# Moving the query, key and value loads of a routed-attention kernel from SyncE's queue to GpSimd's

## What is computed

```python
# layer 1: 3x3 convolution, 64 -> 64, activations quantized to 3 bits, weights to their sign
xq = round(min(1, |x|) * 7) / 7;  wq = sign(W) * mean(|W|);  x = conv(xq, wq) + b
# layer 2: attention over regions, then an MLP
q, k, v = split(layernorm(x) @ wqkv + bqkv)      # as 49 regions of 64 pixels
logits = mean(q over region) @ mean(k over region).T
idx = top_k(logits, 4)                           # 4 regions for each region
kg, vg = k[idx], v[idx]                          # 256 keys and values per region
out = softmax(qh @ kg.T / sqrt(8)) @ vg          # 8 heads of 8 channels
x = x + out @ wo + bo
x = x + gelu(layernorm(x) @ w1 + bm1) @ w2 + bm2
```

## Time and profile before

| | |
|---|---|
| median of 3 runs | 6373.1 us |
| the profiled execution | 6382.89 us |
| its span, first to last instruction | 6381.1 us |
| mean granted TensorE clock | 0.829 |
| busy: TensorE, VectorE, ScalarE, GpSimd | 80%, 57%, 51%, 43% |
| transfers: engines' mean busy share, rate | 31% (SyncE's queue), 81 GB/s |

### The profile page before, as it was taken

How to read it: one execution, slowest core, us unless ns; L and a number is a source line. 1 busy time by engine, 2 the same in 40 slices (tenths; PEclk the granted TensorE clock), 3 DMA queues, 4 the chain that set the end, 5 groups by cost and what they waited for, 6 DMA issues and landing times.

```text
span 6381.1 us, 185291 instructions
## 1 busy us (share of the span) xinstructions
PE 5098.8 (80%) x43666; PEld 3276.5 (51%) x43666; DVE 3650.2 (57%) x8855; ACT 3285.2 (51%) x6282; POOL 2765.1 (43%) x9656
## 2 busy tenths in 40 slices
PE   3488888887878888788788888888888888888888
PEld 1355555555555555555555555555555555555564
DVE  2356565565656565565555655656565555656555
ACT  1246455464555545455464554645455464554646
POOL 1345344353444435444353444535444353443543
PEclk9688788888888788888887888888788887888869
DMA  2433332333334233332333323323242333423311
GB/s 74 96 94 78 82 96 70 92 86 81 85 76 106 66 87 76 85 99 61 99 78 80 94 69 99 81 79 87 74 108 65 87 78 82 104 64 95 85 28 32
DMA packets 832787, 519.79 MB, mean 81 GB/s; under 512 B 592336, under 2 KB 830032, under 8 KB 831600
## 3 DMA queue, kind: packets, MB, share of 16 engines
q1 hardware_dynamic: 831600, 506.70, 31.1%
HBM read 268.80 MB, written 237.63 MB: 79 GB/s over the span
## 4 chain that ended last, share of the span: by engine, by line
PE 35%; SPq 18%; issue 14%; POOL 9%; POOLq 7%; DMA 6%; DVE 4%; DVEq 3%; ACT 2%; ACTq 0%
PE ps L970 9%; PE ps L1000 6%; PE ps L984 5%; SPq L262 5%; POOLq L223 4%; PE ps L863 4%; SPq L292 4%; POOL vg L480 4%; SPq L345 3%; DMA qm<-qk_d 3%; DVEq L223 3%; POOL kg L465 2%; PE ps L956 2%; DMA xin<-in_x 2%; POOL xin L492 2%
## 5 line engine op out<-in xcount | busy, mean ns | idle before, releaser
L705 DVE TENSOR_REDUCE mx<-ps 128x4 f32<-128x1024 f32 x1568 | 1921.7, 1226 | 2055.6 <-PE ps L970 1917.7
L816 ACT ACTIVATE pt<-ps 128x512 f32<-128x512 f32 x3136 | 1696.8, 593 | 1251.9 <-PE ps L984 1229.0
L480 POOL COPY vg<-vs 64x72 f32 x6272 | 1545.6, 246 | 1373.8 <-POOL kg L465 1104.7
L970 PE MATMUL ps<-kg,qm 96*128 96x256 f32 x6272 | 1430.3, 357 | 717.0 <-DMA qm<-qk_d 373.1
L970 PEld LDWEIGHTS ps<-kg,qm 96*128 96x128 f32 x6272 | 1027.4, 220 | 1520.4 <-issue 1361.0
L465 POOL CAST kg<-ks 96x128 fp32r x3136 | 852.1, 296 | 1880.2 <-POOL vg L480 779.6
L984 PE MATMUL ps<-qm,kg 97*128 97x256 f32 x6272 | 1192.9, 318 | 198.6 <-DMA qm<-max_d 143.4
L1000 PE MATMUL ps<-pt,vg 128*32 128x128 f32 x25088 | 1180.4, 312 | 39.4 <-DVE um L695 24.6
L984 PEld LDWEIGHTS ps<-qm,kg 97*128 97x128 f32 x6272 | 1013.4, 222 | 255.5 <-issue 152.0
L1000 PEld LDWEIGHTS ps<-pt,vg 128*32 128x32 f32 x25088 | 673.8, 120 | 306.0 <-issue 91.6
L616 DVE CAST kg<-ks 96x128 fp32r x3136 | 614.1, 237 | 127.0 <-issue 120.5
(11 more groups left out here) (113 smaller groups left out, 4147.5 us busy)
## 6 DMA issues: line engine op xcount, KB each, us to landing
qk_d<-stg SPq DMA_DIRECT2D x448, 224.0 KB, 3.1
qm<-qk_d SPq DMA_DIRECT2D x1792, 42.0 KB
ks<-qk_d SPq DMA_DIRECT2D x224, 336.0 KB, 3.6
vs<-v_d SPq DMA_DIRECT2D x448, 126.0 KB, 3.5
qk_d<-stg SPq DMA_DIRECT2D x112, 448.0 KB, 2.9
xin<-in_x SPq DMA_DIRECT2D x119, 224.0 KB, 2.6
xi_d<-xi SPq DMA_DIRECT2D x112, 224.0 KB, 2.3
max_d<-tr SPq DMA_DIRECT2D x1568, 2.0 KB
```

The lines of the kernel that those rows point to most:

```text
L480: j = pool.tensor_copy(vg[slot][rows, (k // 2) * VW:(k // 2 + 1) * VW], vs[place(m)[0]][rows, bass.ds(region, 1), :].rearrange("p o n -> p ...
L705: v.tensor_reduce(mx[h % 2][:].rearrange("p (g j e) -> p g j e", g=2, j=2)[:, :, :, 0], ps[:, 0:2, :].rearrange("p g (j k) -> p g j k", j= ...
L816: act.activation(pt[m % 2][:, c], ps[:, 2 + c, :], ACT.Exp, scale=float(HD) ** -0.5).then_inc(S["pt_ready"], 1)
L970: i = pe.matmul(ps[:, g, 256 * j:256 * j + 256], qm[c % 2][0:NP3, t, g, 2 * j:2 * j + 2, :].rearrange("p h t -> p (h t)"), kg[slot][0:NP3, ...
```

## The change

- All query, key and value loads move from SyncE's program to GpSimd's: a function `loads`, called at the end of GpSimd's step behind its keys, values and quantization. The queries keep their places (t = 3, 4, 5; 3, 3 and 2 transfers) and their wait.
- Keys and values of an image are 3 + 2 long transfers in place of 7 + 14: the keys one for each of the three terms, the values one for each half of the partitions. One goes out every second step, image 0's from h = 70, image 1's from h = 104. The waits in front of them (all staged, all gathered) move to GpSimd too; SyncE keeps the one before the routing indices, a step earlier.
- `v_d` is laid out by image. Staging is 3 transfers for queries and keys (the slots are taken by high, low and high part) and 4 for values (image by half), over four steps: 2, 2, 2, 1 (offsets 7 to 10).
- The semaphore `staged` becomes `qk_staged`, for which ScalarE waits as before, and `v_staged`, for which VectorE now waits at offset 6 before it overwrites `vstg`.
- In the prologue GpSimd issues the first 8 query loads and the first 5 key and value loads.

```diff
-A_LOAD, B_LOAD = 68, 2
-STAGE_DMAS = 7
-KV_DMAS = 3 * NW
+A_LOAD, B_LOAD = 70, 6
+QK_DMAS, V_DMAS = 3, 4
+KV_DMAS = 5
...
-        v_d = dram("v_d", (PAIRS, RT, R, 2, VW))
+        v_d = dram("v_d", (PAIRS, 2, RT, R, VW))
...
+        def gathered(eng, p, m):
+            for name in ("kd_ready", "kp_ready", "vg_ready"):
+                eng.wait_ge(S[name], p * STEPS + m)
+                settled(eng)
+        def queries(eng, q, c, heads):
+            i, s = c // NW, c % NW
+            src = qk_d[bass.ds(q, 1), i, 0:C, :, ST * s:ST * s + ST].rearrange("o (g h d) q (s t) -> g h (o d q) s t", g=NG, h=HG, s=NW)
+            for g, h in heads:
+                eng.dma_start(qm[c % 2][24 * h:24 * h + 24, :, g, h, :].bitcast(F32), src[g, h]).then_inc(q_loaded[c % 2], 16)
+        def keys_values(eng, q, i, n):
+            if n < 3:
+                src = qk_d[bass.ds(q, 1), i, C:2 * C, n // 2, :].rearrange("o (g c) n -> (o c) g n", g=NG)
+                dst = ks[i][n:NP3:3].rearrange("p g r t -> p g (r t)").bitcast(F32)
+            else:
+                src = v_d[bass.ds(q, 1), i].rearrange("o t r n -> (o t) (r n)")
+                dst = vs[i][64 * (n - 3):64 * (n - 3) + 64].rearrange("p r n -> p (r n)")
+            eng.dma_start(dst, src).then_inc(kv_loaded[i], 16)
+        def loads(eng, p, h, kind):
+            t, c = h % NW, h // NW
+            if t in (3, 4, 5) and live((c + 1) * NW, kind):
+                if t == 3 and not (kind == "lead" and c < 1):
+                    eng.wait_ge(S["st_full"], (p * STEPS + c * NW) * 2)
+                    settled(eng)
+                queries(eng, p + (c + 1) // 14, (c + 1) % 14, [(g, h) for g in range(NG) for h in range(HG)][(t - 3) * 3:(t - 2) * 3])
+            if kind == "loop":
+                if h == A_LOAD:
+                    staged_all(eng, p + 1)
+                    gathered(eng, p, R)
+                if 0 <= h - A_LOAD < 2 * KV_DMAS and (h - A_LOAD) % 2 == 0:
+                    keys_values(eng, p + 1, 0, (h - A_LOAD) // 2)
+            local = h if kind == "lead" else h - STEPS
+            if local >= 0 and kind != "last":
+                if local == B_LOAD and kind != "lead":
+                    gathered(eng, p, STEPS)
+                if 0 <= local - B_LOAD < 2 * KV_DMAS and (local - B_LOAD) % 2 == 0:
+                    keys_values(eng, p if kind == "lead" else p + 1, 1, (local - B_LOAD) // 2)
+        def first_loads(eng):
+            staged_all(eng, 0)
+            queries(eng, 0, 0, [(g, h) for g in range(NG) for h in range(HG)])
+            for n in range(KV_DMAS):
+                keys_values(eng, 0, 0, n)
+        def staged_all(eng, q):
+            eng.wait_ge(S["qk_staged"], (q + 1) * (16 * QK_DMAS * NW))
+            settled(eng)
+            eng.wait_ge(S["v_staged"], (q + 1) * (16 * V_DMAS * NW))
+            settled(eng)
...
-                    def part(term, rows, low):
-                        dst = qk_d[bass.ds(q, 1), :, rows, term, cut].rearrange("o i c n -> (o c) i n")
-                        sp.dma_start(dst, stg[rows, low].bitcast(F32)).then_inc(S["staged"], 16)
...
+                    def part(slot, rows, low):
+                        dst = qk_d[bass.ds(q, 1), :, 0:rows, slot, cut].rearrange("o i c n -> (o c) i n")
+                        sp.dma_start(dst, stg[0:rows, low].bitcast(F32)).then_inc(S["qk_staged"], 16)
+
+                    def value(i, half):
+                        dst = v_d[bass.ds(q, 1), i, :, NW * k + half:NW * k + NW:2].rearrange("o t r n -> (o t) r n")
+                        sp.dma_start(dst, vstg[64 * half:64 * half + 64, 0:4 - half, i, :]).then_inc(S["v_staged"], 16)
...
                     if off == 7:
                         sp.wait_ge(S["l_ready"], q * (2 * NW) + 2 * k + 2)
                         settled(sp)
-                        part(0, slice(0, 2 * C), 0)
-                        part(1, slice(0, C), 0)
-                        part(1, slice(C, 2 * C), 1)
+                        part(0, 2 * C, 0)
+                        part(1, 2 * C, 1)
                     if off == 8:
-                        part(2, slice(0, C), 1)
-                        part(2, slice(C, 2 * C), 0)
+                        part(2, C, 0)
                         sp.wait_ge(S["v_ready"], q * NW + k + 1)
                         settled(sp)
-                        value(0)
+                        value(0, 0)
                     if off == 9:
-                        value(1)
-
-            def staged_all(q):
-
-                sp.wait_ge(S["staged"], (q + 1) * (16 * STAGE_DMAS * NW))
-                settled(sp)
+                        value(0, 1)
+                        value(1, 0)
+                    if off == 10:
+                        value(1, 1)
...
+                loads(pool, p, h, kind)
...
+                first_loads(pool)
...
+                        if not (isinstance(n, int) and n == 0):
+                            v.wait_ge(S["v_staged"], n * (16 * V_DMAS))
                         v.wait_ge(S["v_full"], n + 1)
...
-                            act.wait_ge(S["staged"], n * (16 * STAGE_DMAS))
+                            act.wait_ge(S["qk_staged"], n * (16 * QK_DMAS))
```

More of the change, by code:

```diff
@@ L49 @@
 ROUTE_AT = 62
-A_LOAD, B_LOAD = 68, 2
-STAGE_DMAS = 7
-KV_DMAS = 3 * NW
+A_LOAD, B_LOAD = 70, 6
+QK_DMAS, V_DMAS = 3, 4
+KV_DMAS = 5
 def p_item(h):
-    return [(k, h - P_AT - P_EVERY * k) for k in range(NW) if 0 <= h - P_AT - P_EVERY * k <= 9]
+    return [(k, h - P_AT - P_EVERY * k) for k in range(NW) if 0 <= h - P_AT - P_EVERY * k <= 10]
 def f_item(h):
@@ L168, in build @@
             xq_done xq_ready conv_full xi_ready center_full sq_ready var_full lnv_ready rs_ready xh_ready rx_ready
-            qk_full h_ready l_ready v_full v_ready xi_stored staged
+            qk_full h_ready l_ready v_full v_ready xi_stored qk_staged v_staged
             reg_full reg_ready logit_full lg_ready top_ready topi_ready
@@ L255, in load_x @@
                 sp.dma_start(xin[:], x[bass.ds(q, 1), :, ST * k:ST * k + ST].rearrange("o p n -> (o p) n")).then_inc(S["x_loaded"], 16)
[L257 to L279, removed]
             def stage(q, h):
@@ L288, in stage @@
                         sp.dma_start(xi_d[bass.ds(q, 1), k].rearrange("o p n -> (o p) n"), xi[:].bitcast(F32)).then_inc(S["xi_stored"], 16)
-                    def part(term, rows, low):
-                        dst = qk_d[bass.ds(q, 1), :, rows, term, cut].rearrange("o i c n -> (o c) i n")
-                        sp.dma_start(dst, stg[rows, low].bitcast(F32)).then_inc(S["staged"], 16)
-                    def value(half):
-                        dst = v_d[bass.ds(q, 1), :, NW * k + half:NW * k + NW:2].rearrange("o t r i n -> (o t) r (i n)")
-                        sp.dma_start(dst, vstg[64 * half:64 * half + 64, 0:4 - half].rearrange("p m i n -> p m (i n)")).then_inc(S["staged"], 16)
+                    def part(slot, rows, low):
[4 more added lines that the diff above has]
+                        sp.dma_start(dst, vstg[64 * half:64 * half + 64, 0:4 - half, i, :]).then_inc(S["v_staged"], 16)
                     if off == 7:
@@ L322, in route @@
                 sp.dma_start(idx[i][0:1, :].rearrange("o (y k) -> o y k", k=TOPK), topi[:, i, 0:TOPK]).then_inc(idx_loaded[i], 16)
[L324 to L328, removed]
             def step(p, h, kind):
@@ L345, in step @@
                     sp.dma_start(max_d[h % RING].rearrange("j (b n) -> b j n", n=32), tr[h % 2][0:128:8, :]).then_inc(hopped[h % 2], 16)
[L346 to L351, removed]
                 if kind == "loop":
                     stage(p + 1, h)
-                    if h == A_LOAD - 1:
-                        staged_all(p + 1)
-                        gathered(p, R)
+                    if h == A_LOAD - 2:
+                        gathered(sp, p, R)
                         route(p + 1, 0)
-                    if A_LOAD <= h < A_LOAD + 2 * NW:
-                        image_loads(p + 1, 0, h - A_LOAD)
                     for k, off in x_item(h):
@@ L365, in step @@
                     q = p if kind == "lead" else p + 1
-                    if local == B_LOAD - 1:
+                    if local == B_LOAD - 2:
                         if kind != "lead":
-                            gathered(p, STEPS)
+                            gathered(sp, p, STEPS)
                         route(q, 1)
-                    if B_LOAD <= local < B_LOAD + 2 * NW:
-                        image_loads(q, 1, local - B_LOAD)
                 if kind != "lead":
@@ L397, in before @@
                     load_x(1, k)
-                staged_all(0)
                 route(0, 0)
-                queries(0, 0, [(g, h) for g in range(NG) for h in range(HG)])
-                for n in range(2 * NW):
-                    image_loads(0, 0, n)
             sp.wait_ge(S["zeroed"], 1)
```

## The result

The changed kernel takes 6787.7 us (median of 4 runs, 6779.2 to 6789.4) against 6373.9: ratio 1.064, 95% interval [1.063, 1.066]. Slower, as forecast; 6985 us was predicted, in a range of 6050 to 7800.

The account below looks back on a forecast made before the run. GpSimd was taken to set the pace after the change: a pair of images 421.7 us against 386.0, +35.7, 15 pairs +535, the last pair +78; 6381.1 becomes 6994, against the median 6985 us, range 6050 to 7800.

Parts of the forecast that it names:

- Who binds: GpSimd's own floor is 328 us of a 386.0 us pair of images, so GpSimd sets the pace after the change.
- D: GpSimd's price for issuing one transfer: 1.0 us, estimated from 168 pieces read and written at 3.0 ns each.
- the sum: GpSimd's time per pair of images: 306.7 + 21.5 + 78 + 6 + 9.5 = 421.7 us, against 386.0 before.
- What hides D: GpSimd's 0.81 us of semaphore wait and register loads after the value copies hides issues, 2.4 us a strip.
- The floor: GpSimd's least time per pair: 98 steps, 306.7 us, plus seven strips of quantization, 21.5 us; 328 us.
- The break-even: With GpSimd setting the pace, a pair reaches the old 386 us at D = 0.7; below that the forecast is wrong.
- Rival 1: Faster: D is SyncE's 0.31 to 0.5 us, TensorE's 34.0 us a pair of waits go; 5950 us; chance 0.22.
- Rival 3: No change: D is small, but the stored-values wait moves to VectorE, 35 us a pair; 6375 us; chance 0.05.
- The staging at nothing: Staging and value stores on SyncE, still 7 issues a strip over four steps, were costed at nothing.
- The signs: Profile after: TensorE waiting for GpSimd's keys, not query loads; SyncE nearly always waiting for transposed maxima; ScalarE's 453 us gone.
- The long loads: Ten key and value loads a pair on GpSimd: 6 us; late maxima up to 30 us a pair without cover.

Follow-up runs that it names:

- q_on_act: Changed kernel with query loads issued from ScalarE's queue and the long key and value loads from SyncE; 5951.4 us, 0.936 of the kernel before.
- all_on_sp: Changed kernel with all loads back on SyncE, keeping long key and value loads and the new staging and layout; 6229.2 us, 0.978 of the kernel before.
- q_act_kv_pool: q_on_act with the long key and value loads issued from GpSimd in place of SyncE; 6067.8 us, 0.953 of the kernel before.
- kv_on_sp: Changed kernel with the long key and value loads on SyncE, queries still on GpSimd; 6753.4 us, 1.061 of the kernel before.

## Why the prediction was right, and where its numbers were not

- **Who binds.** Right: GpSimd does after the change. Its floor of 328 us of 386, read as step times and not as busy share, was the point on which the sign hung. The last pair, where nothing but queries was added, went from 322 to 354 us; about 400 was forecast.
- **D.** Mis-sized: 1.0 us taken, 0.65 measured. The estimate that GpSimd passes over pieces at 3 ns each is refuted: 24 pieces 0.536 us, 64 pieces of 12.5 KB 0.582, 168 pieces 0.643, which is 0.5 us an issue and under 1 ns a piece. In the sum this is 14 x 8 x 0.35 = 39 us a pair too much, and 4 more on the ten long loads (0.57 us each).
- **What hides D.** Mis-sized the other way: 0.81 us a step taken, 2.4 a strip; measured 8 x 0.65 - 3.9 = 1.3 a strip. Only beside the last issue of a step does GpSimd's queue get on, and then with waits and not yet with the register load. 14 x 1.1 = 15 us a pair too little.
- **The floor.** Also too low. The quantization's two groups take 12.3 + 9.9 + 2.0 + 1.5 = 25.7 us with their idle time, about the 31.0 assumed; but 306.7 + 14 x 3.9 + 25.7 is 387 of the 410 us of a pair. The timeline names most of the rest. A plain step, without issue, quantization or long load, lasts 3.14 us in the median, but 3.27 in the mean (683 steps), for single register loads take up to 1.95 us in place of 0.50; that is 98 x 0.13 = 13 us. The steps with issues last 4.11 us (two) and 5.00 us (three) in the mean, 4.3 us a strip more than plain ones in place of 3.9, which is 6 us. The floor of 3.13 us a step was the best case and not the mean. In all, the pair of 421.7 us in the sum is 12 too long, because too dear an issue and too low a floor partly cancel.
- **The break-even.** Here the prediction was lucky. With the true D its own formula gives 306.7 + 21.5 + 14 x (5.2 - 2.4) + 10 x 0.25 + 9.5 = 379 us, against 386 before: some 1% faster in all. That it would be wrong with D under 0.7 us was written down, and D was 0.65: by its own working the forecast should have failed, and the kernel is still 6.4% slower. The threshold was wrong; it lay too high because of the hiding and of the floor.
- **Rival 1** said what SyncE's relief is worth when GpSimd pays nothing: 5871 to 6028 us. q_on_act, which has that relief at no cost to GpSimd, took 5951. That is 26 us a pair and not the 34 of TensorE's waits, and GpSimd's pace is what stops it.
- **Rival 3**: no wait moved to VectorE. The staging at nothing was right.
- **The signs.** ScalarE's 453 us are gone, and the gaps are 2.31 and 2.48 us in two of the three steps. Two signs came out otherwise: TensorE waits for query loads more than before (67.2 us a pair) and next to never for GpSimd's keys (2.4 us), and SyncE waits 2046 us for the transposed maxima, under a third of the span, and 1677 us for their stores to land.
- **The long loads.** Priced at 6 us of GpSimd's time plus "up to 30 us a pair" for maxima beside them without GpSimd as cover. With GpSimd last they cost 34 us in all, 2 a pair; without that cover, at every second step, 116 to 135 us, 7 to 8 a pair.
- **Two rules of the Trainium skill.** The 0.4 us that its table puts between the two paths to the first byte (the Trainium skill, "DMA: Bandwidth & Descriptors", Specifications) would have given D = 0.7: close to the 0.65, for whatever reason, and better than my estimate. No landing shows it: the long key loads land in 5.9 us from GpSimd and in 6.3 from SyncE (all_on_sp). The lock of GpSimd by VectorE's copies (the Trainium skill, "SBUF — State Buffer", SBUF: two separate sides) shows little: 1792 issues lie between 628 and 873 ns, median 643, beside VectorE's two copies a step.

## What to carry to other kernels

Before work is moved to an engine, its real step is to be timed start to start, with the register loads and self-waits in it; "43% busy" was 85% full. A transfer issued from GpSimd costs its engine 0.5 to 0.65 us here, nearly whatever its size, and only the last of a group hides; ScalarE's queue took the same issues at 0.31 us, and the kernel became 6.4% faster than before. Large loads that GpSimd issues are best held further apart than they take to land: at 6.4 us apart the small transfers on the critical chain were late, at some 9.7 us most of the loss was gone. From SyncE, where they were some 7.5 us apart or more already, the wider spacing made the kernel 53 us slower.

## What the runs showed of the hardware

- An issue on GpSimd is an engine instruction: 0.51 to 0.54 us for 24 pieces, 0.55 to 0.58 for 64, 0.64 for 168. On SyncE and ScalarE the 168 pieces take 0.31.
- A 2 KB store was seen as landed 1.7 us after its issue where no long load was in its way, and 3.8 to 5.8 us after it beside a load of 0.8 MB issued on another queue (q_act_kv_pool). On the same queue it was 3.7 to 5.7 us (q_on_act).
- The changed kernel moves 361,746 packets in place of 832,787, and of those through GpSimd's queue 70,144 carry 212 MB, although the query loads alone are 1792 x 168 = 301,056 pieces of 256 bytes. With the queries on SyncE the total is 626,963. With the query loads alone on GpSimd's queue (kv_on_sp) it carries 57,344 packets, 32 for each load of 168 pieces. So pieces are packed together on the software queue. What that is worth in time was not tested.
